# Another order of the units on the five engine queues of a sequence-layer kernel, with an order of its own for the end and the first gram between the weights

## What is computed

```python
x_act = tanh(x)
static_out = einsum('bld,ed->ble', x_act, W)      # also the values v
q = k = heads(x_act); v = heads(static_out)       # 16 heads of 16
# per sequence and head, token after token:
S = lam * S
u = beta * (v_t - S^T k_t)
S = S + k_t u^T
o_t = S^T q_t
y = static_out + o
x1 = layernorm(x + (layernorm(y) * gamma + ln_beta))
h  = silu(x1 @ wg^T) * (x1 @ wu^T)
out = layernorm(x1 + h @ wd^T)
```

## Time and profile before

| what | value |
|---|---|
| median of 3 runs | 1757.72 us (1757.12 to 1758.14) |
| the profiled execution, its own time | 1760.27 us |
| its span | 1758.5 us |
| mean granted TensorE clock | 0.855 of full speed |

### The profile page before, as it was taken

One profiled execution on the slowest core, in us unless ns is written; L12 is line 12 of the kernel. 1 busy time (PEld: TensorE's weight loads), 2 busy tenths in 40 slices (PEclk: granted clock), 3 DMA queues, 4 the chain that ended last, 5 costly groups with the idle time before them and its releaser, 6 DMA issues.

```text
span 1758.5 us, 53677 instructions
## 1 busy us (share of the span) xinstructions
PE 1384.7 (79%) x21032; PEld 1077.1 (61%) x21032; DVE 1398.9 (80%) x3461; ACT 1104.1 (63%) x2357; POOL 802.2 (46%) x1106
## 2 busy tenths in 40 slices
PE   4357888897888888888888888888889887888764
PEld 3345666675666666666666676666667666666542
DVE  5578888888888888888888888888888887888741
ACT  3236666666666766676677666667666665676544
POOL 6023454444445544444455444445444443544542
PEclk9568889988888989888889988888998888898777
DMA  4555544555654456555455555654455555445200
GB/s 126 109 102 114 110 115 111 121 106 114 127 120 107 115 119 110 117 115 127 106 120 115 121 106 112 126 106 119 113 124 112 113 114 110 120 110 115 49 25 24
DMA packets 701325, 190.98 MB, mean 109 GB/s; under 512 B 620944, under 2 KB 688528, under 8 KB 701072
## 3 DMA queue, kind: packets, MB, share of 16 engines
q1 hardware_dynamic: 701072, 187.56, 50.1%
HBM read 103.55 MB, written 67.11 MB: 97 GB/s over the span
## 4 chain that ended last, share of the span: by engine, by line
PE 25%; SPq 23%; DVE 21%; DMA 15%; ACT 9%; issue 6%; POOL 1%; ACTq 0%; POOLq 0%; DVEq 0%
PE pc L181 11%; SPq L947 6%; DMA scr_t<-t 6%; SPq L956 6%; SPq L1003 4%; SPq L990 4%; ACT v L683 4%; DMA scr_x<-xt 3%; PE pf L226 3%; PE pf L215 2%; DMA kb<-k 2%; PE pu L252 2%; SPq L1013 2%; DVE S L384 2%; DVE Sp L381 2%
## 5 line engine op out<-in xcount | busy, mean ns | idle before, releaser
L884 POOL TENSOR_TENSOR hlo<-gate,hhi 128x512 f16<-128x512 f32 x192 | 228.7, 1193 | 330.5 <-ACT hhi L715 330.1
L181 PE MATMUL pc<-R,tb 128*128 128x32 f16 x4096 | 158.0, 188 | 130.5 <-DVE R L367 115.7
L181 PEld LDWEIGHTS pc<-R,tb 128*128 128x128 f16 x4096 | 147.5, 118 | 147.6 <-DVE R L367 128.8
L181 PE MATMUL pc<-S,e 128*128 128x32 f16 x4096 | 157.1, 186 | 73.9 <-DVE S L388 73.9
L181 PEld LDWEIGHTS pc<-S,e 128*128 128x128 f16 x4096 | 151.5, 118 | 91.1 <-DVE S L388 83.8
L278 PE MATMUL pd<-wd_t,hhi 128*128 128x256 f16 x768 | 176.1, 276 | 13.9 <-DVE xr L486 8.4
L181 PEld LDWEIGHTS pc<-U,kb 128*128 128x128 f16 x4096 | 155.2, 118 | 44.9 <-DVE U L375 42.7
L215 PEld LDWEIGHTS pf<-xb,e 128*128 128x128 f16 x4096 | 152.4, 118 | 49.5 <-DMA e<-scr_x 31.7
L181 PE MATMUL pc<-U,kb 128*128 128x32 f16 x4096 | 159.6, 190 | 22.0 <-DVE U L375 22.0
L215 PE MATMUL pf<-xb,e 128*128 128x32 f16 x4096 | 156.3, 192 | 25.8 <-DMA e<-scr_x 23.7
L278 PE MATMUL pd<-wd_t,hlo 128*128 128x256 f16 x768 | 175.7, 275 | 0.0
(11 more groups left out here) (124 smaller groups left out, 3285.7 us busy)
## 6 DMA issues: line engine op xcount, KB each, us to landing
xa<-L_attn_x SPq DMA_DIRECT2D x128, 128.0 KB
scr_x<-xt SPq DMA_DIRECT2D x64, 256.0 KB, 2.2
xb<-scr_x SPq DMA_DIRECT2D x256, 64.0 KB, 2.8
e<-scr_x SPq DMA_DIRECT2D x256, 64.0 KB, 3.7
scr_g<-gs SPq DMA_DIRECT2D x32, 512.0 KB, 3.5
gh<-scr_g SPq DMA_DIRECT2D x32, 512.0 KB, 3.5
kb<-k SPq DMA_DIRECT2D x512, 32.0 KB, 2.2
scr_t<-t SPq DMA_DIRECT2D x64, 256.0 KB, 4.5
```

The lines of the kernel that those rows point to most:

```text
L181: last = pe.matmul(pc2[:, :, cols], stationary(h, a), moving[:, :, cols], start=a == 0, stop=a == 1)
L884: pool.tensor_tensor(hlo[:, t, :], gate[:, t % 2, :], hhi[:, t, :], ALU.subtract).then_inc(SEM["hl"], 1)
```

## The change

Every list is written in another order. No operation is added to the units or taken away, and no size changes. Places in a step that the text comes back to:

- SP: the second `kb` load now stands ahead of the store of the inverse, the two halves of that store are apart, and the residual load stands between the store of half 0 and the load of half 0. The load of x stands ahead of the store of the gram.
- PE: the static product of window 0 stands ahead of the first inverse product, the whole of the down projection behind it. The other static products stand one at a time between the groups of windows 1 and 2, and the transposes of the keys come a stage sooner.
- ACT: `act_static_out` of group 0 stands ahead of the update of window 2. All four first-norm calls stand ahead of the update of window 3. The first scaling of the keys moves from the start of a step to the end of the step before.
- DVE: columns 13 and 14 of the inversion and the state of window 3 stand in another place, the first scaling of the keys stands ahead of the store of the inverse, and the key norms ahead of the update of window 0.
- `LAST` is `NS`, so the step functions end with step 31, and the rest is written out in `pe_tail`, `dve_tail`, `act_tail`, `pool_tail` and `sp_tail`. There the x1 of the last unit lies in `xa` (`x1_of`), a tile that is free by then, so its first norm need not wait for the last norm of unit 30.
- Start: w_down is loaded last, and its six transposed pairs follow the gram of unit 0, which stands ahead of step -1 now. The zeroing of `kb` on POOL goes ahead of that of the second `E`. SP's and ACT's places of step -1 are those of every step, so x of unit 1 is loaded ahead of the store of the gram of unit 0.

```diff
-        FIRST, LAST = -1, NS + 3
+        FIRST, LAST = -1, NS
+
+        def x1_of(q):
+
+            return xa if q == NS - 1 else xr
...
         def sp_step(sp, s, p):
+            if live(s):
+                sp_load_kb(sp, s, p, 0)
             if live(s + 1) and s >= 0:
                 sp_store_keys(sp, s + 1, 1 - p, 0)
                 sp_store_keys(sp, s + 1, 1 - p, 1)
                 sp_spread_packed_keys(sp, s + 1, 1 - p)
                 sp_spread_keys(sp, s + 1, 1 - p)
+            if live(s):
+                sp_load_kb(sp, s, p, 1)
+                sp_store_inverse(sp, s, p, 0)
             if live(s - 1):
                 sp_load_residual(sp, s - 1, 1 - p)
             if live(s):
-                sp_store_inverse(sp, s, p, 0)
+                sp_load_inverse(sp, s, p, 0)
                 sp_store_inverse(sp, s, p, 1)
-                sp_load_inverse(sp, s, p, 0)
-                sp_load_kb(sp, s, p, 1)
-            if live(s + 1):
-                sp_store_gram(sp, s + 1, 1 - p)
-            if live(s):
-                sp_load_inverse(sp, s, p, 1)
-            if live(s + 1):
-                sp_load_gram(sp, s + 1, 1 - p)
             if live(s + 2):
                 sp_load_x(sp, s + 2, p)
+            if live(s + 1):
+                sp_store_gram(sp, s + 1, 1 - p)
+            if live(s):
+                sp_load_inverse(sp, s, p, 1)
+            if live(s + 1):
+                sp_load_gram(sp, s + 1, 1 - p)
             if live(s - 2):
                 sp_store_out(sp, s - 2, p)
-            if live(s + 1):
-                sp_load_kb(sp, s + 1, 1 - p, 0)
...
+            act_gram(eng, 0, 0, 0)
...
+            for j in range(ND, NJ):
+                eng.wait_ge(s_ps, j + 1)
+                eng.activation(jobs[j][1], ps[j % 2], ACT.Copy).then_inc(s_wt, 1)
             eng.wait_ge(s_c, N_SETUP)
+            act_scale_keys(eng, 0, 0, 0)
             all_steps(eng, act_step)
+            act_tail(eng)
```

More of the change, by code:

```diff
@@ L245, in pe_transpose_x1 @@
             for n in range(NW):
-                last = pe.transpose(pg[half][:, n * P:(n + 1) * P], xr[:, n, half * P:(half + 1) * P], ident[:, :])
+                last = pe.transpose(pg[half][:, n * P:(n + 1) * P], x1_of(q)[:, n, half * P:(half + 1) * P], ident[:, :])
             last.then_inc(SEM["x1p"], 1)
@@ L340, in pe_step @@
             if live(s):
-                pe_keys_by_update(pe, s, p, 2)
+                pe_inverse_by_rest(pe, s, p, 2)
             if live(s + 2):
@@ L345, in pe_step @@
             if live(s):
+                pe_keys_by_update(pe, s, p, 2)
                 pe_keys_by_state(pe, s, p, 3)
@@ L517, in dve_step @@
                 dve_rest(dve, s, p, 0)
+            if live(s + 1):
+                dve_scale_keys(dve, s + 1, 1 - p, 1)
+            if live(s + 1) and s >= 0:
+                dve_gram(dve, s + 1, 1 - p, 2)
             if live(s - 2):
@@ L532, in dve_step @@
                 dve_add_ffn(dve, s - 2, p, 1)
+            if live(s + 1) and s >= 0:
+                dve_gram(dve, s + 1, 1 - p, 3)
             if live(s):
@@ L569, in dve_step @@
                 dve_transpose_keys(dve, s + 2, p, 1)
+            if live(s):
+                dve_state(dve, s, p, 2)
+            if live(s + 1):
+                dve_invert(dve, s + 1, 1 - p, range(3, 5))
             if live(s):
@@ L576, in dve_step @@
                 dve_update(dve, s, p, 3)
-            if live(s + 1):
-                dve_invert(dve, s + 1, 1 - p, range(8, 9))
             if live(s - 1):
@@ L1086, in _ @@
             eng.dma_start(wu_nat, w_up.rearrange("(t p) d -> p t d", p=P)).then_inc(s_ldn, 16)
-            for a in range(2):
-                eng.dma_start(wd_nat[a], w_down[a * P:(a + 1) * P, :]).then_inc(s_ldn, 16)
             eng.dma_start(gamma[:, :], bc(ln_gamma, D)).then_inc(s_ldb, 16)
@@ L1096, in _ @@
             sp_spread_keys(eng, 0, 0)
+            for a in range(2):
+                eng.dma_start(wd_nat[a], w_down[a * P:(a + 1) * P, :]).then_inc(s_ldd, 16)
             all_steps(eng, sp_step)
+            sp_tail(eng)
             eng.wait_ge(SEM["out"], NS * PER["out"])
@@ L1185, in _ @@
             assert n[0] == N_SETUP
+            dve_gram(eng, 0, 0, 0)
+            dve_gram(eng, 0, 0, 1)
+            dve_gram(eng, 0, 0, 2)
+            dve_gram(eng, 0, 0, 3)
+            eng.wait_ge(s_ldd, 32)
+            for nat, w32 in zip(wd_nat, wd32):
+                eng.tensor_copy(w32, nat).then_inc(s_cast, 1)
             eng.wait_ge(s_ldb, 32)
             all_steps(eng, dve_step)
+            dve_tail(eng)
         @block.tensor
@@ L1199, in _ @@
             last.then_inc(s_wps, 1)
-            eng.wait_ge(s_cast, 4)
-            for j, (srcs, _) in enumerate(jobs):
+            eng.wait_ge(s_cast, 2)
+            for j in range(0, ND):
                 if j >= 2:
                     eng.wait_ge(s_wt, j - 1)
-                for a, w32 in enumerate(srcs):
+                for a, w32 in enumerate(jobs[j][0]):
+                    last = eng.transpose(ps[j % 2][:, a * P:(a + 1) * P], w32, ident[:, :])
+                last.then_inc(s_ps, 1)
+            pe_gram(eng, 0, 0, 0, range(0, 8))
+            pe_gram(eng, 0, 0, 0, range(8, 16))
+            pe_gram(eng, 0, 0, 1, range(0, 8))
+            pe_gram(eng, 0, 0, 1, range(8, 16))
+            pe_gram(eng, 0, 0, 2, range(0, 8))
+            pe_gram(eng, 0, 0, 2, range(8, 16))
+            pe_gram(eng, 0, 0, 3, range(0, 8))
+            pe_gram(eng, 0, 0, 3, range(8, 16))
+            eng.wait_ge(s_cast, 4)
+            for j in range(ND, NJ):
+                if j >= 2:
+                    eng.wait_ge(s_wt, j - 1)
+                for a, w32 in enumerate(jobs[j][0]):
                     last = eng.transpose(ps[j % 2][:, a * P:(a + 1) * P], w32, ident[:, :])
```

375 lines of the change are left out of this document (264 added, 111 removed).

## The result

The changed kernel takes 1761.59 us (median of 20 runs, 1755.53 to 1766.71), the kernel before, in runs between them, 1756.38 us (20 runs, 1748.86 to 1762.98). The ratio is 1.0036, 95% interval 1.0024 to 1.0048: slower by 0.36%, where the forecast was 1743 us and faster. The clock is not the reason: the mean granted TensorE clock is 0.870 of full speed in the profile after, for 0.855 before.

What follows compares the result with a forecast made beforehand. No engine alone bounds it; two nearly equal cycles, recurrence and inverse, set the step. Start +11, end -14 and 30 steps of -0.45 gave -16.5, 1741.2 us from the median 1757.72, put at 1743; range 1720 to 1768.

Steps and rivals of the forecast that it cites:

- Inverse side: Step, SP's chain from keys' store through `E`, inverse store and `tb` to PE: -0.8 us, of which -0.45 carried to the mean.
- From there to the start of `E`: SP, from the store of the keys at T+22.6 to `E`: 7.1 us, T being the step's first inverse product.
- Recurrence side: Step, state recurrence with PE's work between its groups: -1.15 us in sum, from 50.93 to 49.8.
- Item 1: PE, first inverse product to second state product: 16 more down matmuls behind the inverse product, +0.66 us.
- Item 2: PE, second state product to window 1's inverse product: no static matmuls between any more, 3.83 to 2.81, -0.9 us.
- Item 3: ACT, first `act_static_out` ahead of window 2's update waits for the output store's landing: +0.5 us, bounds nothing and 1.55.
- Item 4: PE, transposes of x1 no longer wait for ACT's norm, and `dve_transpose_x1` comes at once: -1.15 us.
- Item 5: PE ahead of the next first inverse product: 16 down matmuls gone, half a gram group and a static product added, -0.25 us.
- Start and end: First inverse product 11 us later (+3 to +13); unit 31's feed-forward 24 behind unit 30's for 38.3, -14 (-18 to -8).
- C: Rival, slower: ACT stalls before window 2's update until the output store lands; period 51.3 to 51.8, 1767 to 1782 us, chance 0.22.
- B: Rival: step unchanged, `tb`'s landing takes back the store's gain, residual's price 2.3 us moving to it; 1754.7 us, chance 0.24.
- A: The forecast itself: period shorter by 0.2 to 0.9 us, 1728 to 1752 us, chance 0.42.

Runs made afterwards that it cites:

- 9: `a_kb4`: changed kernel with only the first four of the eight transfers of the second `kb` load; 0.9924, 1743.12 us.
- 7: `b_res`: kernel before with the residual load moved behind both stores of the inverse; 0.9890, 1738.44 us.
- 6: `a_res`: changed kernel with the residual load back ahead of the store of the inverse's half 0; 1.0840, 1907.18 us.
- 11: Changed kernel with `act_static_out` of group 0 behind the update of window 2 again; 1.0103, 1774.67 us.

## Why the prediction was wrong

**What bounds a step.** Right that two cycles are nearly equal and that the inverse side would be the later; 9 shows it. Wrong in treating the other as having 0.7 us in hand, and wrong in subtracting from the mean of 50.93 for both. That mean held waits for SP, for `tb` and for `kb`. With fewer of them the old order takes 50.2 (7).

**Inverse side, the step that failed.** "From there to the start of `E` it is 569.20-562.10 = 7.1", and with it "SP is at the store of the inverse at T+40.6, for T+40.76 now ... -0.2", and +0.2 for DVE. The step in the rows was a slow one for the store: 28 steps before have it at 40.1, and those after at 41.5, so +1.4 where the prediction had 0. Of these 1.4 us, 0.7 is the base, 0.8 the 7.9 us to `E` for 7.1, 0.2 the keys' store at 22.9 for 22.6, less 0.3 for the issues behind `E`, 10.8 for 11.1. With +0.2 for DVE the prediction's own links add up to 50.7, which is 0.2 below the mean of 50.93; it went on with 50.5, a part of a difference to a step of 51.50. "From the store to the `tb` load ... -1.5": measured -1.1, for the base was again a slow one (5.34 for a mean of 4.6). "From the `tb` load ... +0.7": -0.1 against the mean before, and 0.7 at most (6). Its ends of -1.9 and +0.8 don't follow from its own bounds, which give -2.2 and +1.5. In all this side is 51.2.

**Recurrence side, the second error.** Item 1, +0.66: measured +0.68. Item 2, -0.9: measured -0.36. The 3.83 us came from one step with 0.85 idle in it; over 28 steps the stretch was 3.29, and is 2.93. Item 3, +0.5: windows 1 to 3 came 0.57 later, but not for its reason, so the size was luck. The wait for the output store, to be read beside the earlier trace rows, is 2 us more over the whole run:

```profile
  ACT v L709: 5.7, 7
```

Of the 0.57, 0.27 lie between the state product and the inverse product of window 2 and 0.18 behind the latter, where static products and the transposes of the keys stand now; that was not tried by itself. Item 4, -1.15: measured -1.1. Item 5, -0.25: from the start of the transposes of x1 to T it is 22.0 in `a_kb4`, for 21.5 in `b_res`, so +0.5. The prediction moved the gram 2 us forward and put its wait for `E` at nothing; PE waits 0.6 us a step for it. This side is 50.7, not 49.8.

**Start and end.** +11 was +12.4, -14 was -15.0, with unit 31's feed-forward 25.6 behind unit 30's for the 24 forecast. That `gh` can be loaded only 5.6 us after `scr_g` behind the load of x, for 3.4, was not in the sum.

**Rivals.** C lies nearest in time (1767 at its lower end, B 1754.7, measured 1761.59) and in the period (51.3 at its lower end, measured 51.2), but not for its reason: one sign of being wrong did show, a wait of 1.9 us at ACT's `v<-pf`, yet all 7 waits are 5.7 us, and 11 excludes it. B's price was not moved to `tb`. A had the right side as the later one, and its length too short.

## What to carry to other kernels

Where a DMA queue's issues follow each other without a gap, its length from the first late input to the last output is a bound like any engine's: add up its links from means over many steps, not from one, and compare totals, not differences, before believing a gain of less than their spread. Look at every load that the queue feeds to another engine, not at the last alone: here PE waited for `E` as well as for `tb`. A store that something waits for should not stand right behind large loads on its queue; here one such call was worth 1.1%. A call's place can rest on another's: before moving one alone, look who waits for its buffer.

## What the runs showed that was not expected

- A small store right behind loads of 512 KB lands in about 4.5 us, and in 2.2 without them; eight small loads behind the same 512 KB show no price against the kernel before (6.2 and 6.3 us from the first issue to use), and 0.7 us at most against `a_res` (5.5).
- The same list of eight `kb` loads took 5.3 us to issue in one place of a step (818.06) and 6.1 in another (837.18); over 28 steps the two places differ less, 5.6 and 5.9.
- Half of a load left out, 2.9 us of issue in a step of 51, shortened the kernel by 1.1%; the same scaling of 0.8 us moved on the busiest engine, DVE, changed nothing.
- In `a_res` PE waited 3.7 us a step, and what stood behind the wait took 1.6 us more, at a granted clock of 0.60 for 0.99.
